# Layer 0 attention: score masks added by VectorE in two of four query blocks, softmax sums inverted in packed form by way of DRAM

## What is computed

```
q = (x @ wq).reshape(b, s, 32, 16)
k, v = (x @ wk), (x @ wv), 8 heads each, repeated 4 times
scores = einsum('bihd,bjhd->bhij', q, k) * SCALE
scores = where(causal, scores, finfo.min)
attn = softmax(scores, axis=-1)
out = einsum('bhij,bjhd->bihd', attn, v).reshape(b, s, 512) @ wo
```

## Time and profile before

| | |
|---|---|
| median of three runs | 952.16 us |
| the profiled execution, its own time | 952.0 us |
| its span, first to last instruction | 950.1 us |
| PE busy | 877.9 us, 92% of the span |
| DVE busy | 693.6 us, 73% |
| ACT busy | 533.1 us, 56% |
| POOL busy | 189.5 us, 20% |
| chain that ended last | PE 75%, DVE 9%, issue 5%, POOL 4%, ACT 3%, DMA 2%, SPq 1% |
| mean granted TensorE clock | 0.976 |

### The profile page before, as it was taken

The page is one execution under the profiler, slowest core; times in us unless marked ns, Lnnn a source line. Parts: engine busy times, 40 slices in busy tenths (PEclk is TensorE's granted clock), DMA queues, the critical chain, the costliest instruction groups (busy, mean ns, idle before and its releaser), DMA issues.

```text
span 950.1 us, 13799 instructions
## 1 busy us (share of the span) xinstructions
PE 877.9 (92%) x5224; PEld 693.3 (73%) x5224; DVE 693.6 (73%) x892; ACT 533.1 (56%) x707; POOL 189.5 (20%) x197
## 2 busy tenths in 40 slices
PE   2799999999988889898999999999988999999996
PEld 1567667666667668686888888788866888888885
DVE  3835698888888768778677777587887866667842
ACT  3313667657654434486666657477727766666830
POOL 3002555666557213300000000000040000000004
PEclk9798999999898999999999999999999999999998
DMA  9588565655535103105233333133312333332202
GB/s 309 171 243 152 67 109 69 113 101 66 103 78 179 34 12 105 51 22 147 83 106 103 102 99 113 46 105 95 111 45 67 111 104 97 99 101 67 67 1 89
DMA packets 40610, 93.59 MB, mean 99 GB/s; under 512 B 7000, under 2 KB 10072, under 8 KB 40544
## 3 DMA queue, kind: packets, MB, share of 16 engines
q1 hardware_dynamic: 36416, 87.35, 36.6%
q10 hardware_dynamic: 4128, 5.36, 1.7%
HBM read 77.98 MB, written 2.11 MB: 84 GB/s over the span
## 4 chain that ended last, share of the span: by engine, by line
PE 75%; DVE 9%; issue 5%; POOL 4%; ACT 3%; DMA 2%; SPq 1%; POOLq 0%; DVEq 0%; ACTq 0%
PE PS L1509 15%; PE PS L1510 14%; PE PS L1511 14%; PE PS L1815 5%; PE PS L1814 5%; PE PS L1813 5%; PE PS L1607 4%; PE PS L1639 2%; PE PS L1622 2%; DVE MX L1295 2%; POOL QS L731 2%; DMA WM<-in_WM 1%; POOL X L715 1%; PE PS L1531 1%; DVE ACC L1157 1%
## 5 line engine op out<-in xcount | busy, mean ns | idle before, releaser
L837 ACT ACTIVATE PL<-CODE 128x1024 f32<-128x1024 int32 x200 | 201.9, 1057 | 60.3 <-DVE ACC L1157 55.7
L1509 PE MATMUL PS<-HH,WRH 128*128 128x512 f32 x448 | 176.7, 394 | 11.2 <-DVE HL L1116 4.7
L1510 PE MATMUL PS<-HH,WRL 128*128 128x512 f32 x448 | 175.6, 392 | 0.0
L1511 PE MATMUL PS<-HL,WRH 128*128 128x512 f32 x448 | 175.6, 392 | 0.0
L715 POOL TENSOR_TENSOR X<-X,SCR 128x512 f32<-128x512 f32 x32 | 42.6, 1343 | 560.2 <-DVE SCR L1142 560.1
L1157 DVE SCALAR_TENSOR_TENSOR ACC<-PL,ACC 128x1024 f32<-128x1024 f32 x100 | 123.1, 1231 | 8.4
L879 ACT ACTIVATE PT<-PS 128x512 f32<-128x512 f32 x160 | 85.5, 602 | 67.3 <-PE PS L1622 45.1
L1295 DVE TENSOR_REDUCE MX<-PS 128x2 f32<-128x256 f32 (+3 forms) x128 | 100.5, 820 | 29.4 <-PE PS L1609 14.8
L1509 PEld LDWEIGHTS PS<-HH,WRH 128*128 128x128 f32 x448 | 84.9, 189 | 31.2 <-issue 6.3
L731 POOL TENSOR_TENSOR QS<-ident,MX 64x256 fp32r<-64x256 f32 x128 | 93.6, 732 | 66.6 <-DVE MX L1295 60.0
L1511 PEld LDWEIGHTS PS<-HL,WRH 128*128 128x128 f32 x448 | 84.8, 189 | 18.0
(11 more groups left out here) (225 smaller groups left out, 1528.2 us busy)
## 6 DMA issues: line engine op xcount, KB each, us to landing
CODE<-in_CODES SPq DMA_DIRECT2D x50, 512.0 KB, 3.5
SCALE<-in_SCALES SPq DMA_DIRECT2D x100, 256.0 KB, 4.0
WM<-in_WM SPq DMA_DIRECT2D x12, 1024.0 KB, 5.9
QS<-FH SPq DMA_DIRECT2D x32, 128.0 KB, 4.1
QS<-FL SPq DMA_DIRECT2D x32, 128.0 KB, 5.1
X<-in_X ACTq DMA_DIRECT2D x2, 1024.0 KB, 12.3
GAB<-gates SPq DMA_DIRECT2D x4, 512.0 KB, 3.8
out_x<-X ACTq DMA_DIRECT2D x8, 256.0 KB, 2.0
```

The source lines that it names most:

```text
L837: nc.scalar.activation(PL[:, n % 3], CODE[:, p % 2], ACT.Prelu, scale=scale, bias=bias, alpha=alpha).then_inc(s_plane, 1)
L1509: nc.tensor.matmul(dst, lh, rh, start=start and k == 0, stop=False)
L1510: nc.tensor.matmul(dst, ll, rh, start=False, stop=False)
L1511: ins = nc.tensor.matmul(dst, lh, rl, start=False, stop=stop and k == KC - 1)
```

## The change

In the units with n % 4 of 0 or 1 PE leaves out the mask product of the scores. There DVE runs four instructions in place of two, each over one head: they add the columns of a constant CMASK (zeros and then the mask), write the result back to PSUM and give its maximum. CMASK is built once by POOL. The mask product of the transposed scores stays.

For pairs 0 to 5, SP copies one row of each 16 equal sums, 8 x 512 of them, into RC, 128 partitions x 16 (`pack_sums`, two DMAs); DVE inverts RC in one short instruction; SP stores it in DRAM in the swapped order (`store_inverses`, two DMAs) and reads it back 16-fold into DENS (`spread_inverses`, one DMA of 128 x 512). The shuffle and the two reciprocals of these pairs go. The product with the numerators moves from unit 8p + 17 to 8p + 24 (pair 5 to unit 61). The decoding steps move from slots (2, 4, 6) to (0, 1, 5), and pair 5's rounding from unit 60 to 62.

```diff
--- before.py
+++ after.py
@@ -78,12 +78,19 @@
 
 LOW_RANK_AT = [(0, KC - 1), (1, 1), (1, KC - 1)]
 PAIRS = GROUPS // 2
-ROUND_AT = {41: 0, 46: 1, 49: 2, 54: 3, 58: 4, 60: 5, 63: 6}
+ROUND_AT = {41: 0, 46: 1, 49: 2, 54: 3, 58: 4, 62: 5, 63: 6}
 SPLIT_AT = {46: 0, 51: 1, 54: 2, 59: 3}
 SWAP = list(range(HD, 2 * HD)) + list(range(HD))
 
 
 STEPS = len(CAPS) + 1
+
+
+ADDED_MASK = (0, 1)
+
+
+PACK_AT = {2 * pair + 5: pair for pair in range(B * PAIRS - 2)}
+SPREAD_AT = {min(2 * pair + 6, B * GROUPS - 1): pair for pair in range(B * PAIRS - 2)}
 
 
 SECOND_AT = 2
@@ -115,7 +122,7 @@
 
 def step_at(n):
 
-    slots = (2, 4, 6)
+    slots = (0, 1, 5)
     if not 0 <= n < B * GROUPS * TB or n % 8 not in slots:
         return None
     return divmod(n // 8 * len(slots) + slots.index(n % 8), STEPS)
@@ -247,6 +254,8 @@
         MR = sb("MR", [P, D], F32)
         gab0 = at[0]
         GAB = sb("GAB", [P, B, D], F32)
+        CMASK = sb("CMASK", [P, TB * P], F32, gab0)
+        RC = sb("RC", [P, S // HD], F32, gab0 + 4 * TB * P)
         MCOL = sb("MCOL", [P, 2, 4, KC, B], F32)
         ident = sb("ident", [P, P], F32)
         maskR = sb("maskR", [P, P], F32R)
@@ -359,6 +368,7 @@
         XN = [sb(f"XN{n}", [P, TB, D], F32, R0 + off * K) for n, off in enumerate((40, 40, 40, 40))]
         XM = [sb(f"XM{n}", [P, 2, D], F32, R0 + off * K) for n, off in enumerate((72, 16, 80, 48))]
 
+        INV = nc.dram_tensor("inverses", (REP, 2, S), F32, kind="Internal").ap()
         GD = nc.dram_tensor("gates", (4, B, D), F32, kind="Internal").ap()
 
         PS = ctx.enter_context(nc.psum_tensor("PS", [P, 8, 512], F32))
...
@@ -535,6 +549,31 @@
                 sp.wait_ge(s_free, J[last_gated(i - 1)] + 1)
             sp.wait_ge(s_gd, 16 * B)
             sp.dma_start(GAB[:], GD[i:i + 1].to_broadcast([P, B, D])).then_inc(s_gab, 16)
+
+        def pack_sums(sp, pair):
+
+            b, c = divmod(pair, PAIRS)
+            sp.wait_ge(s_odd, 2 * pair + 2)
+            if pair:
+                sp.wait_ge(s_rs, 32 * pair)
+            for u in range(2):
+                sp.dma_start(RC[64 * u:64 * u + 64], DEN[HD * u:P:2 * HD, c, b * S:(b + 1) * S]).then_inc(s_dn, 16)
+
+        def store_inverses(sp, pair):
+
+            sp.wait_ge(s_ri, pair + 1)
+            if pair:
+                sp.wait_ge(s_rb, 16 * pair)
+            for u in range(2):
+                sp.dma_start(INV[:, 1 - u], RC[64 * u:64 * u + 64]).then_inc(s_rs, 16)
+
+        def spread_inverses(sp, pair):
+
+            sp.wait_ge(s_rs, 32 * (pair + 1))
+            if pair:
+                sp.wait_ge(s_div, pair)
+            sp.dma_start(DENS[:], INV.rearrange("h u s -> (h u) s").unsqueeze(1).to_broadcast([GROUPS, HD, S])
+                         ).then_inc(s_rb, 16)
 
         def load_stack(sp, n):
 
@@ -621,7 +660,15 @@
                                  ).then_inc(s_wm[n % 3], 16)
 
             for n in range(B * GROUPS):
+                if n in PACK_AT:
+                    pack_sums(sp, PACK_AT[n])
+                if n - 1 in PACK_AT:
+                    store_inverses(sp, PACK_AT[n - 1])
                 load_stack(sp, n)
+                if n == B * GROUPS - 1:
+                    store_inverses(sp, PACK_AT[n])
+                if n in SPREAD_AT:
+                    spread_inverses(sp, SPREAD_AT[n])
                 if n == STACKS:
                     sp.wait_ge(s_mr, 1)
                     for b in range(B):
@@ -674,6 +721,11 @@
             pool.wait_ge(s_free, J["norm", 0, B - 1, KC - 1] + 1)
             for odd in range(2):
                 link(nc.gpsimd.memset(V[:, :, odd::2, 1 - odd, :], 1.0))
+            pool.wait_ge(s_mm, J["modcol", 1, COLS[-1]] + 1)
+            pool.wait_ge(s_const, 16 * 3)
+            link(nc.gpsimd.memset(CMASK[:, 0:(TB - 1) * P], 0.0))
+            nc.gpsimd.tensor_copy(CMASK[:, (TB - 1) * P:], maskB[:]).then_inc(s_ones, 1)
+            pool.wait_ge(s_ones, 3)
             pool.wait_ge(s_mm, J["v", B - 1] + 1)
             for i in range(1, STACKS):
                 link(nc.gpsimd.memset(KN[i][64:P].bitcast(F32), -1.0))
@@ -1226,8 +1278,14 @@
                 cols = slice(half * (S // 2), (half + 1) * (S // 2))
                 link(nc.vector.reciprocal(DENS[:, cols], DENS[:, cols]))
 
+            def invert_packed(pair):
+                dve.wait_ge(s_dn, 32 * (pair + 1))
+                nc.vector.reciprocal(RC[:], RC[:]).then_inc(s_ri, 1)
+
             def divide(pair):
                 b, c = divmod(pair, PAIRS)
+                if pair < B * PAIRS - 2:
+                    dve.wait_ge(s_rb, 16 * (pair + 1))
                 cols = slice(b * S, (b + 1) * S)
                 nc.vector.tensor_tensor(NUM[:, c, cols], NUM[:, c, cols], DENS[:], ALU.mult).then_inc(s_div, 1)
                 dve.wait_ge(s_div, pair + 1)
@@ -1292,6 +1350,14 @@
                     if n >= 2:
                         dve.wait_ge(s_dg, 2 * (n - 1))
                     w = (n % TB + 1) * P
+                    if n % TB in ADDED_MASK:
+                        if n == 0:
+                            dve.wait_ge(s_ones, 3)
+                        for h in (2 * pair, 2 * pair + 1):
+                            ins = nc.vector.tensor_tensor_reduce(PS[:, h, 0:w], PS[:, h, 0:w], CMASK[:, TB * P - w:], 1.0,
+                                                                 MASKED, ALU.add, ALU.max, MX[:, n % 2, h:h + 1])
+                        ins.then_inc(s_mx, 1)
+                        continue
                     nc.vector.reduce_max(MX[:, n % 2, 2 * pair:2 * pair + 2], PS[:, 2 * pair:2 * pair + 2, 0:w], AX_X
                                          ).then_inc(s_mx, 1)
                 if step_at(n) and step_at(n)[1] < STEPS - 1:
@@ -1300,13 +1366,18 @@
                     gate_values()
                 if pair_at(n, 4) is not None:
                     copy_odd(pair_at(n, 4))
-                if pair_at(n, 5) is not None:
-                    swap_sums(pair_at(n, 5))
-                for half, unit in enumerate((5, 6) if n >= 60 else (7, 8)):
-                    if pair_at(n, unit) is not None:
-                        invert(half)
-                if pair_at(n, 7 if n >= 60 else 9) is not None:
-                    divide(pair_at(n, 7 if n >= 60 else 9))
+                if pair_at(n, 7) in PACK_AT.values():
+                    invert_packed(pair_at(n, 7))
+                if pair_at(n, 16) in range(B * PAIRS - 3):
+                    divide(pair_at(n, 16))
+                if n == B * GROUPS * TB - 3:
+                    divide(B * PAIRS - 3)
+                    swap_sums(B * PAIRS - 2)
+                    invert(0)
+                if n == B * GROUPS * TB - 2:
+                    invert(1)
+                if n == B * GROUPS * TB - 1:
+                    divide(B * PAIRS - 2)
                 if n in SPLIT_AT:
                     split_heads(SPLIT_AT[n])
 
@@ -1604,10 +1675,11 @@
                     if n >= 1:
                         pe.wait_ge(s_mx, 2 * (n - 1) + half + 1)
                     for h in (2 * half, 2 * half + 1):
-                        nc.tensor.matmul(PS[:, h, 0:(ic + 1) * P], QS[:, q % STACKS, h, ic * P:(ic + 1) * P],
+                        ins = nc.tensor.matmul(PS[:, h, 0:(ic + 1) * P], QS[:, q % STACKS, h, ic * P:(ic + 1) * P],
                                          KS[:, q % STACKS, 0:(ic + 1) * P], start=True, stop=True)
-                        ins = nc.tensor.matmul(PS[:, h, ic * P:(ic + 1) * P], identR, maskR[:], start=False, stop=True,
-                                               skip_group_check=True)
+                        if ic not in ADDED_MASK:
+                            ins = nc.tensor.matmul(PS[:, h, ic * P:(ic + 1) * P], identR, maskR[:], start=False, stop=True,
+                                                   skip_group_check=True)
                     ins.then_inc(s_s, 1)
 
             def transposed(n):
```

More of the change, by code:

```diff
@@ L434, in build @@
         s_gd = sem("gates_stored")
+        s_dn = sem("denominators_packed")
+        s_ri = sem("denominators_inverted")
+        s_rs = sem("inverses_stored")
+        s_rb = sem("inverses_spread")
         s_gab = sem("gates_spread")
```

## The result

The changed kernel took 975.09 us, the median of 4 runs (974.13 to 980.06), the kernel before in the same comparison 952.28 us (950.35 to 953.62): a ratio of 1.0252, with a 95% interval from 1.0212 to 1.0291. It is slower by 22.8 us. The forecast was 967.5 us with a range of 948 to 981 us, so the side is right and 7.6 us are missing from the size. The profiled execution has a span of 973.8 us and a mean granted clock of 0.963, where it was 950.1 us and 0.976.

A forecast was written before the change was run, and what follows sets the result against it. The prediction took a ring of in-order engines, set by order as much as amount, to bound layer 0's attention. Savings -6, ACT's order +11, late codes +7.5 and clock +3 gave +15.5 us on 952 us: 967.5 us, range 948 to 981.

The forecast's parts named there:

- What bounds the stage: Attention of layer 0: a ring of in-order engines, none free or full, set by order of work as much as amount.
- ACT's order, +11 us: Moved decoding slots put 13 curve passes of 1.0 us into ACT's gapless units 5 to 7: +11 us.
- Late codes +7.5 and clock +3 us: Pieces 4 and 5 wanted earlier, loads unmoved: +4.5 and +3.0 us; a second low-clock hole on PE: +3 us.
- The savings, -6 us: Of 14.1 us less on PE and 10.8 us less on DVE, 6 us reach the end, 1 per heavy group.
- +13.5 us on DVE: Masks added in units 0 and 1 of a group lengthen DVE's maxima by 13.5 us, bounds +4.5 and +27.5.
- the longer maxima stand in the ring: Bound of the savings: PE waits for DVE's later maxima, a loss of 4 us.
- A wait for the landing of each is covered: SP's five added DMAs per pair: pack to inverse has about three units, 8 us; a codes load lands in 4.1 us.
- The savings win: Rival: 14 us of PE and 11 us of DVE count, ACT hides its curves; 10 us faster, 942 us; chance 0.16.
- they cancel: Rival: PE's gains -14, slots half hidden +5.5, codes and clock +8 us, giving 951.5 us; chance 0.07.
- SP's queue becomes the bound: Rival: an added DMA costs SP 1.3 us of issuing, not 0.63; codes come later, +9 us, 976.5 us; chance 0.15.
- Nothing behind the stage changes: Everything after the attention of layer 0 is only shifted in time, at no cost of its own.
- The rule on accumulators: DVE's adding maximum may be two instructions; if the second is as long as the smallest row, some 5 us later.

The follow-up runs named there:

- early codes: Loads of code pieces 4 and 5 issued one stack earlier, behind stacks 10 and 13 instead of 11 and 14; in the kernel before alone: 949.83 us, ratio 0.9985.

## Why the prediction was right, and what in it was not

**What bounds the stage: shown.** I read a ring of in-order engines set by order, and one line of slots that changes no work cost 24.5 us, while less work on PE and 13 us less on DVE gained nothing at the end.

**ACT's order, +11 us: 14.3 us.** The rows named beforehand came: passes between the exponentials of units 6 and 7, the weight loads' wait at 40.3 us ("over 25"), a light group of 11.75 us ("over 11"). The term is 3.3 us too small. ACT's part is at least 8.2 us; up to 6.1 us lie elsewhere, for which I had allowed "some 3 us more" only in the upper bound. That the sum of the passes came so near is in part luck. I had counted each pass as 1.0 us of delay that PE feels; PE's standing still grew by 6.1 us, and 10.3 us came from a lower clock, which I had tied to late codes alone. And I had put ACT's folds at nothing, one of which makes the longest stop, by way of POOL.

**Late codes +7.5 and clock +3 us: 10.0 us together.** ACT waited 3.87 us for piece 4 ("some 4") and 6.76 us for piece 5 ("5"), and a second and a third hole opened. The sum is right within half a microsecond. As a mechanism the clock term was too narrow: the clock fell behind other stops as well.

**The savings, -6 us: this step failed.** It is the term that was mis-sized. Beside the slots the savings measure 975.09 - 976.54 = -1.5 us, which is inside the spread of the runs, with early codes +0.6 us, and with old slots and early codes +4.7 us. I let 6 us through because DVE's work in the heavy groups "costs at most 3 us" each. With the packing alone the group from unit 12 got 0.8 us shorter and the light one behind it 0.6 us longer:

- *Masks.* The counts were right, and +13.5 us on DVE was near: at 128 columns one head follows another after 0.25 us, at 256 after 0.385 us (294.67 us, then 295.06 us, for one), so 64 x (0.25 + 0.385) = 40.6 us replace 29.9 us, +10.7 us. On PE, 9.4 us less work met 6.1 us more of standing still, and the 3.2 us that were left did not reach the end. I had named this ("the longer maxima stand in the ring") only as the lower bound.
- *Packing.* "A wait for the landing of each is covered" by three units was wrong for the pack: it covers the landing from the unit in which the sums are ready, but SP issues the pack when its queue gets there, up to the very unit that wants the result. In the changed kernel this is one wait of 3.8 us, at 185.18 us; with the old slots and early codes it is three, of 11.0 us. The first low clock above (0.66, PE busy 5.42 of 10 us) has two causes: PE stands 2.29 us behind this wait and then 3.50 us for POOL, and the second stop is there without any packing.

The terms by the runs are 14.3 + 10.0 - 1.5 = +22.8 us. They add up to the measured loss because they are differences of the same medians, so that is no test of them; mine were 11 + 10.5 - 6 = +15.5 us. The 7.3 us between the two sums are 3.3 us of the slots and 4.5 us of the savings, both on the same side, less 0.5 us of the codes.

**Rivals.** *The savings win* and *they cancel* fell with the result, and the slots alone show why. *SP's queue becomes the bound*: its price is refuted, since an added DMA takes 0.6 us of issuing (RC 0.55 us; two in 1.25 us), not 1.3 us. Its time, 976.5 us, lies near the result by accident. SP's waits for a stack's room were to fall to near 10 us; they rose to 22.5 us in the row that was 14.8 us, because the loop behind which it waits got slower. The queue had air on the average, and was late all the same where the codes stood in it. That unit 60 would come 13 us late was too little: 22.3 us. "Nothing behind the stage changes" holds within 1.6 us.

**The rule on accumulators.** The trace has a row of its own for the read of the accumulator, 0.14 us, behind each adding maximum. That is as the Trainium skill (VectorE: DVE Perf Modes, section "Two Vector instructions with no wait between them") says: such an operation is two instructions. But the result was not 5 us later for it, since the read overlaps the next head's instruction. Start to start a head takes 0.25 us, against 0.20 us worked out without an accumulator: 0.05 us, near the 0.07 us taken and not the 0.18 us.

## What to carry to other kernels

In a ring of in-order engines look for the stretch in which an engine has no gap, and keep every piece of work that nobody wants yet out of it: the slots that put 13 passes of 1.0 us and a fold there cost 14.3 us, and slots that put the passes into the gap behind it gained 5.1 us. Count a stop of PE twice, once for itself and once for the clock behind it. Work taken off engines of such a ring turns for the most part into waiting: here it was worth 3.8 us up to unit 24, and one hand-over that came late took that back. A load that stands last in a long queue has to be moved with its consumer, and slack for a hand-over is counted from when the queue issues it, not from when its data are ready.

## What the runs showed of the hardware

A maximum that is also an output costs less than its rows say: 0.32 us and 0.14 us of busy time at 128 columns, but 0.25 us from head to head. After 6 us in which PE did nothing (260 to 266 us, granted clock already 0.71 in the mean) it was given 0.50 for the next 4 us, with 3.02 us of busy time in them. So a wait of 6.76 us for one load of 512 KB costs more than itself: in these 4 us half of PE's pace is lost as well. Shorter stops cost clock too. With the slots and early codes, PE's longest stop is 4.32 us, the stage's mean clock is 0.93, and the same 1871 products keep PE busy 187.24 us in place of 176.91 us.
